# Flamingo block, latent attention: rotated query rows and folded matrix as two f16 parts, the partner sums placed a step earlier, the Exp table loaded ahead

## The reference, cut to what matters

```python
q_hk  = (hidden_q @ Wq.T).reshape(Bv, Sv, H, K)
q_big = einsum('bshk,hkq->bshq', q_hk, w_kc_q)
q_big = _apply_rope(q_big, sin_q, cos_q)        # x * cos + rotate_half(x) * sin
kv_r  = _apply_rope(kv_c, sin_k, cos_k)
q_r   = einsum('bshq,hqr->bhsr', q_big, W_qr)
k_r   = einsum('bld,hdr->bhlr', kv_r, W_kr)
attn  = softmax(einsum('bhsr,bhlr->bhsl', q_r, k_r), axis=-1)
ctx_c = einsum('bhsl,bld->bhsd', attn, kv_r)
ctx   = einsum('bhsd,hkd->bhsk', ctx_c, w_kc_kv)   # then @ Wo.T
```

## Time and profile before

| | |
|---|---|
| median of 3 runs | 469.99 us (468.45 to 471.33) |
| the profiled execution, its time | 470.19 us |
| its span, first to last instruction | 468.4 us |
| mean granted TensorE clock | 0.989 |
| first layer with its loads | 0 to about 144 us |
| attention | about 144 to 360 us |
| experts | about 360 to 468 us |

### The profile page before, as it was taken

How to read it: one execution, slowest core, us unless ns; L and a number is a source line. 1 busy time by engine, 2 the same in 40 slices (tenths; PEclk the granted TensorE clock), 3 DMA queues, 4 the chain that set the end, 5 groups by cost and what they waited for, 6 DMA issues and landing times. The chain is left out here.

```text
span 468.4 us, 8841 instructions
## 1 busy us (share of the span) xinstructions
PE 431.7 (92%) x2723; PEld 275.3 (59%) x2723; DVE 305.8 (65%) x886; ACT 251.6 (54%) x628; POOL 187.7 (40%) x190
## 2 busy tenths in 40 slices
PE   5895999989988999999999999999998997899997
PEld 2574777776744655555555555555565863644476
DVE  3989799964266767667775766867643759446612
ACT  3593436445335767776677676676665241145500
POOL 3450304040516546565555646545633006444000
PEclk9996999999999999999999999999999999999999
DMA  7733000000105233433424343212200898588202
GB/s 247 220 94 98 3 0 2 1 1 22 47 0 131 65 94 78 108 90 75 100 74 110 75 99 86 67 45 58 56 2 1 241 309 251 163 185 255 68 29 91
DMA packets 61448, 43.81 MB, mean 94 GB/s; under 512 B 22955, under 2 KB 54502, under 8 KB 61414
## 3 DMA queue, kind: packets, MB, share of 16 engines
q1 hardware_dynamic: 60646, 41.04, 32.9%
q0 software_dynamic: 768, 2.36, 2.5%
HBM read 27.25 MB, written 2.23 MB: 63 GB/s over the span
## 5 line engine op out<-in xcount | busy, mean ns | idle before, releaser
L1200 POOL TENSOR_TENSOR W1T<-W1T,inv 128x512 f32<-128x512 f32 x64 | 66.5, 1039 | 76.1 <-DVE inv L1250 75.8
L1144 ACT ACTIVATE W1T<-ps,low 128x256 f32<-128x256 f32 x128 | 59.5, 470 | 29.5 <-DVE low L1244 29.5
L275 POOL TENSOR_TENSOR rot<-rot 128x512 f32<-128x512 f32 x48 | 61.0, 1271 | 30.5 <-DMA rot<-rot 30.3
L1244 DVE TENSOR_REDUCE low<-ps 128x2 f32<-128x512 f32 x64 | 44.1, 689 | 39.6 <-PE ps L1062 39.1
L1070 PE MATMUL ps<-ident,W1T 128*128 128x128 f32 x256 | 41.1, 283 | 2.4 <-POOL W1T L1200 1.6
L1070 PEld LDWEIGHTS ps<-ident,W1T 128*128 128x128 f32 x256 | 27.7, 141 | 25.3 <-issue 20.3
L1152 ACT ACTIVATE W2T<-ps 128x512 f32<-128x512 f32 x64 | 38.2, 597 | 7.9 <-PE ps L1070 5.9
L255 DVE TENSOR_TENSOR rot<-ps,sinq 128x512 f32<-128x512 f32 x48 | 33.2, 691 | 13.3 <-PE ps L242 11.2
L242 PE MATMUL ps<-XH,CH 128*128 128x512 f16 x96 | 36.4, 379 | 0.9 <-DVE XL L859 0.9
L242 PE MATMUL ps<-XL,CH 128*128 128x512 f16 x96 | 36.4, 379 | 0.0
L242 PE MATMUL ps<-XH,CL 128*128 128x512 f16 x96 | 36.4, 379 | 0.0
(11 more groups left out here) (246 smaller groups left out, 867.2 us busy)
## 6 DMA issues: line engine op xcount, KB each, us to landing
rot<-rot SPq DMA_DIRECT2D x64, 128.0 KB, 2.3
rot<-rot SPq DMA_DIRECT2D x64, 64.0 KB, 2.0
EGU<-in_L_ffn_W_gate_dram SPq DMA_DIRECT2D x8, 384.0 KB, 5.7
EGU<-in_L_ffn_W_up_dram SPq DMA_DIRECT2D x8, 384.0 KB, 5.8
ED<-in_L_ffn_W_down_dram SPq DMA_DIRECT2D x8, 384.0 KB, 5.8
rot<-in_L_ffn_W_dram SPq DMA_DIRECT2D x2, 1024.0 KB, 8.1
WQ<-in_L_xattn_Wq_dram SPq DMA_DIRECT2D x8, 256.0 KB, 2.9
WO<-in_L_xattn_Wo_dram SPq DMA_DIRECT2D x8, 256.0 KB, 3.1
```

Source lines behind the costliest of these rows:

```text
L275: pool.tensor_tensor(g.RO[:, n, x, :], g.RO[:, n, x, :], g.TC[x][:, :], ALU.add).then_inc(g.sum_ok, 1)
L1144: e = act.activation(PB[t % 2][:, h, :], g.ps[:, SC + t % 2, h * S:(h + 1) * S], ACT.Exp, bias=low[:, t % 2, h:h + 1], scale=-1.0, accum_o ...
L1200: pool.tensor_tensor(PB[t % 2][:, :, :], PB[t % 2][:, :, :], inv[:, t % 2, :].unsqueeze(2).broadcast_to([P, 2, S]), ALU.mult).then_inc(nor ...
L1244: dve.tensor_reduce(low[:, t % 2, :], g.ps[:, SC + t % 2, :].rearrange("p (h s) -> p h s", h=2), AX.X, ALU.min).then_inc(low_ok, 1)
```

## The change

- Folded matrix: fold 4 joins `FOLD_SPLIT`; M is kept as two f16 parts MH and ML, scaled by UP = 64. ACT writes MH, and DVE (POOL in the first layer) the rest. In the stage DVE does it in step 7, behind the last inverse.
- Query rows: the sum of a group stands in RS, which has room for three groups and not six. ACT copies it to f16 (`rotated_high`, into RH), POOL subtracts that from RS and writes the f16 rest (`rotated_low`, into RL, in the space of XN).
- Context product: three terms (high x high, high x low, low x high) in f16 where one f32 product was. The factor 1/(UP UP) is taken out when the result is kept and when its rest is taken, for which DVE now uses scalar_tensor_tensor.
- A swap waits for `ro_low` of the group that had its place in RS, three groups earlier, and no longer for the context product.
- Order in the steps: sum 2 moves from step 4 to 3, sum 3 stays in 5, sum 4 in 6, and sum 5 goes from step 0 of the next pair to step 7. In steps 3 and 7 the low of an earlier group stands in front of the sum, in steps 4 and 6 the lows stand behind. ACT does high 0 and 1 in step 3, high 2 at the start of step 5 ahead of the exponentials, high 3 and 4 in step 7, high 5 at the start of step 1 of the next pair. POOL does low 5 in step 0, behind the normalisation.
- First layer's end: high and low of groups 0 to 2 are added on ACT and POOL, the first context product stands behind fold 0, and ACT issues an exponential of one element, with its table load, behind the first context keep.
- `bn_aggr` counts on the semaphore of `bn_stats`.

```diff
-FOLD_SPLIT = (0, 1, 5)
+FOLD_SPLIT = (0, 1, 4, 5)
...
     if f == 4:
-        return act.activation(g.M[u][:, :, :], o[:, 0:QT * DC], ACT.Copy, scale=1.0 / UP)
+        return act.activation(g.MH[u][:, :, :], o[:, 0:QT * DC], ACT.Copy, scale=UP)
...
-ROPE0, QC0, QCPS0, SUM0 = 2, 1, 2, QT
+ROPE0, QC0, QCPS0, SUM0, LOW0 = 2, 1, 2, QT, QT
...
     sp.wait_ge(g.sin_ok, GROUPS_Q * q + (k + 1))
-    sp.wait_ge(g.qc_ps, 2 * q + (n - 1 + QCPS0))
+    sp.wait_ge(g.ro_low, GROUPS_Q * q + (k - QT + 1 + LOW0))
...
-    pool.tensor_tensor(g.RO[:, n, x, :], g.RO[:, n, x, :], g.TC[x][:, :], ALU.add).then_inc(g.sum_ok, 1)
+    pool.tensor_tensor(g.RS[:, x, :], g.RS[:, x, :], g.TC[x][:, :], ALU.add).then_inc(g.sum_ok, 1)
+
+
+def rotated_high(act, g, q, k):
+
+    n, x = k // QT, k % QT
+    act.wait_ge(g.sum_ok, GROUPS_Q * q + (k + 1 + SUM0))
+    act.wait_ge(g.qc_ps, 2 * q + (n - 1 + QCPS0))
+    act.activation(g.RH[:, n, x, :], g.RS[:, x, :], ACT.Copy).then_inc(g.ro_high, 1)
+
+
+def rotated_low(pool, g, q, k):
+
+    n, x = k // QT, k % QT
+    pool.wait_ge(g.ro_high, GROUPS_Q * q + (k + 1))
+    pool.tensor_tensor(g.RL[n][:, x, :], g.RS[:, x, :], g.RH[:, n, x, :], ALU.subtract).then_inc(g.ro_low, 1)
 
 
 def context_product(pe, g, q, u, n):
 
-    pe.wait_ge(g.sum_ok, GROUPS_Q * q + (QT * n + QT + SUM0))
+    pe.wait_ge(g.ro_low, GROUPS_Q * q + (QT * n + QT + LOW0))
     pe.wait_ge(g.qc_ok, 2 * q + (n + QC0))
-    for h in range(2):
-        pe.matmul(g.ps[HI[h], QP, :], g.M[u][:, h, :], g.RO[:, n, h, :], start=True, stop=False)
-    for h in range(2):
-        mm = pe.matmul(g.ps[HI[h], QP, :], g.M[u][HI[h], 2, :], g.RO[HI[h], n, 2, :], start=False, stop=True)
+    terms = split(g.MH[u], g.ML[u], g.RH[:, n], g.RL[n])
+    for m, (mx, rx) in enumerate(terms):
+        for h in range(2):
+            pe.matmul(g.ps[HI[h], QP, :], mx[:, h, :], rx[:, h, :], start=(m == 0), stop=False)
+    for m, (mx, rx) in enumerate(terms):
+        for h in range(2):
+            mm = pe.matmul(g.ps[HI[h], QP, :], mx[HI[h], 2, :], rx[HI[h], 2, :], start=False, stop=(m == 2))
     mm.then_inc(g.qc_ps, 1)
...
                 if b == B - 1 and n >= 1:
                     add_partners(pool, g, 0, n - 1)
+                    if n == 1:
+                        rotated_low(pool, g, 0, 0)
+        for k in range(1, QT):
+            rotated_low(pool, g, 0, k)
...
         pe.wait_ge(gelu_ok, UNITS * B)
-        context_product(pe, g, 0, 0, 0)
         pe.wait_ge(x2_ok, 2 * B)
         pe.wait_ge(g.attention.credit, 1)
         next_fold(0)
+        context_product(pe, g, 0, 0, 0)
         second_norm(B - 1)
...
+                if b == B - 1 and n == 2:
+                    rotated_high(act, g, 0, 0)
+        for k in range(1, QT):
+            rotated_high(act, g, 0, k)
         norm_root(act, g, n2, B - 1)
...
         context_keep(act, g, 0, 0, 0)
+        act.activation(primed[:, :], g.gate[0:1, 0:1], ACT.Exp)
...
-    SUMMED = {1: 0, 2: 1, 4: 2, 5: 3, 6: 4}
+    SUMMED = {1: 0, 2: 1, 3: 2, 5: 3, 6: 4, 7: 5}
+    LOW_FIRST = (3, 7)
+    HIGH = {3: (0, 1), 7: (3, 4)}
+    LOW = {3: (0,), 4: (1, 2), 6: (3,), 7: (4,)}
...
         def step(p, u, t, asks, folds):
+            if asks and t == 5:
+                rotated_high(act, g, p + 1, QT - 1)
             softmax(p, t)
...
             if folds and t >= 3:
                 fold(p + 2, u, t - 3)
+            if asks:
+                for k in HIGH.get(t, ()):
+                    rotated_high(act, g, p + 1, k)
...
         def cross(p, u, t, asks, folds):
 
+            if t == 1:
+                rotated_high(act, g, p, GROUPS_Q - 1)
             softmax(p, t)
...
         def step(p, u, t, asks, folds):
             normalise(p, t)
-            if asks and t in SUMMED:
-                summed(p + 1, SUMMED[t])
+            if asks:
+                if t in SUMMED and t not in LOW_FIRST:
+                    summed(p + 1, SUMMED[t])
+                for k in LOW.get(t, ()):
+                    rotated_low(pool, g, p + 1, k)
+                if t in LOW_FIRST:
+                    summed(p + 1, SUMMED[t])
...
         def cross(p, u, t, asks, folds):
             step(p, u, t, asks, folds)
             if t == 0:
-                summed(p, GROUPS_Q - 1)
-
-        for k in range(QT, GROUPS_Q):
-            summed(0, k)
-        pairs(pool, step, cross)
+                rotated_low(pool, g, p, GROUPS_Q - 1)
+
+        summed(0, QT)
+        for k in range(QT, GROUPS_Q - 1):
+            summed(0, k + 1)
+            rotated_low(pool, g, 0, k)
+        pairs(pool, step, cross, head)
...
             inverse(p, t)
+            if folds and t == LAST:
+                fold(p + 2, u, FOLDS - 2)
```

More of the change, by code:

```diff
@@ L71, in norm_stats @@
     for t in range(n * q, n * q + n):
-        dve.wait_ge(nm.stats, t + 1)
-        dve.bn_aggr(g.mv[:, t, :], g.stat[:, t, :]).then_inc(nm.aggr, 1)
-    dve.wait_ge(nm.aggr, n * q + n)
+        dve.wait_ge(nm.stats, n * q + t + 1)
+        dve.bn_aggr(g.mv[:, t, :], g.stat[:, t, :]).then_inc(nm.stats, 1)
+    dve.wait_ge(nm.stats, 2 * n * (q + 1))
     dve.tensor_scalar(g.var[:, n * q:n * q + n], g.mv[:, n * q:n * q + n, 1], LN_EPS, None,
@@ L177, in fold_keep, with fold_parts @@
     if f == 4:
-        return act.activation(g.M[u][:, :, :], o[:, 0:QT * DC], ACT.Copy, scale=1.0 / UP)
+        return act.activation(g.MH[u][:, :, :], o[:, 0:QT * DC], ACT.Copy, scale=UP)
     return act.activation(g.NH[:, bass.ds(r, 1), :], o[:, 0:D], ACT.Copy, scale=UP)
+def fold_parts(g, r, u, f):
+    if f < 2:
+        return g.CH[u][:, f, :], g.CL[u][:, f, :], 2 * DQ
+    if f == 4:
+        return g.MH[u][:, :, :], g.ML[u][:, :, :], QT * DC
+    return g.NH[:, r, :], g.NL[:, r, :], D
 def fold_rest(dve, g, r, u, f, o):
-    hi, lo, w = ((g.CH[u][:, f, :], g.CL[u][:, f, :], 2 * DQ) if f < 2 else
-                 (g.NH[:, bass.ds(r, 1), :], g.NL[:, bass.ds(r, 1), :], D))
+    hi, lo, w = fold_parts(g, bass.ds(r, 1), u, f)
     return dve.scalar_tensor_tensor(out=lo, in0=o[:, 0:w], scalar=UP, in1=hi, op0=ALU.mult, op1=ALU.subtract)
@@ L292, in context_keep @@
     for h in range(2):
-        act.activation(g.Q[h][u][HI[h], 512 * n:512 * n + 512], g.ps[HI[h], QP, :], ACT.Copy).then_inc(g.qc_hi, 1)
+        act.activation(g.Q[h][u][HI[h], 512 * n:512 * n + 512], g.ps[HI[h], QP, :], ACT.Copy,
+                       scale=1.0 / (UP * UP)).then_inc(g.qc_hi, 1)
 def context_rest(dve, g, q, u, n):
@@ L300, in context_rest @@
     for h in range(2):
-        m = dve.tensor_tensor(g.Q[h][u][HI[1 - h], cols], g.ps[HI[h], QP, :], g.Q[h][u][HI[h], cols], ALU.subtract)
+        m = dve.scalar_tensor_tensor(out=g.Q[h][u][HI[1 - h], cols], in0=g.ps[HI[h], QP, :], scalar=1.0 / (UP * UP),
+                                     in1=g.Q[h][u][HI[h], cols], op0=ALU.mult, op1=ALU.subtract)
     m.then_inc(g.qc_ok, 1)
@@ L344, in stage_first_layer @@
     FS = sb("FS", [P, 2 * DQ])
+    primed = sb("exp_primed", [1, 1])
     FILL = 8 - TOP_BLK
@@ L430, in _ @@
         pool.memset(g.ident[:, :], 0.0).then_inc(id_zero, 1)
-        for start, v in ((g.rope_ok, ROPE0), (g.qc_ok, QC0), (g.qc_ps, QCPS0), (g.sum_ok, SUM0)):
+        for start, v in ((g.rope_ok, ROPE0), (g.qc_ok, QC0), (g.qc_ps, QCPS0), (g.sum_ok, SUM0),
+                         (g.ro_low, LOW0)):
             pool.sem_inc(start, v)
@@ L643, in first_queries @@
             pe.wait_ge(xl_ok, 2)
-            pe.wait_ge(fold_b, 2)
+            pe.wait_ge(fold_b, len(FOLD_SPLIT))
             pe.wait_ge(g.rope_ok, k + ROPE0)
@@ L1005, in stage_latent_attention, with pairs @@
     LAST = NT - 1
-    def pairs(eng, step, cross):
+    def pairs(eng, step, cross, head=None):
         for t in HEAD:
-            step(0, 0, t, True, False)
+            (head or step)(0, 0, t, True, False)
         with eng.Fori(0, (PAIRS - 2) // 2, 1) as it:
@@ L1172, in step, with head @@
                 turned(p, t - 1)
+        def head(p, u, t, asks, folds):
+            for k in range(QT, GROUPS_Q):
+                if t == min(1, k - QT):
+                    rotated_high(act, g, 0, k)
+            step(p, u, t, asks, folds)
         def cross(p, u, t, asks, folds):
+            if t == 1:
+                rotated_high(act, g, p, GROUPS_Q - 1)
             softmax(p, t)
@@ L1186, in _ @@
             fold(1, 1, f)
-        pairs(act, step, cross)
+        pairs(act, step, cross, head)
         turned(PAIRS - 1, LAST)
@@ L1205, in step, with head @@
             normalise(p, t)
-            if asks and t in SUMMED:
-                summed(p + 1, SUMMED[t])
+            if asks:
[5 more added lines that the diff above has]
+                    summed(p + 1, SUMMED[t])
+        def head(p, u, t, asks, folds):
+            step(p, u, t, asks, folds)
+            if t == 0:
+                rotated_low(pool, g, 0, GROUPS_Q - 1)
         def cross(p, u, t, asks, folds):
@@ L1949, in build @@
             g.CH, g.CL = two("CH", [P, KT, 2 * DQ], F16), two("CL", [P, KT, 2 * DQ], F16)
```

(8 more changed lines are left out.)

14 lines of the change are left out of this document (7 added, 7 removed).

## The result

The changed kernel is slower. Its median is 477.91 us (476.40 to 478.89, four runs), that of the kernel before, timed beside it, 470.66 us (468.45 to 471.70, four runs): ratio 1.0127, 95% interval 1.0086 to 1.0169. Medians are over all executions; the ratios leave out executions in a slower state, over 1.5% above the fastest of the same kernel. The prediction, 468.6 us with a range of 461 to 475, is wrong in size and in sign.

What follows compares the result with a forecast made beforehand. PE's order of work was taken to bound the attention stage. Inner pairs -4.7, start +0.5 and last transition +2.8 gave -1.4 us, so 468.6 us from a profiled 470.19, range 461 to 475.

Steps and rivals of the forecast that it cites:

- start, pair 0, steps 0 to 2: Start of the attention stage: POOL's new low parts delay the first transposes and product, less the product's saving; +0.5 us.
- six inner pairs, step 3 to step 2: Inner attention pairs, step 3 to the next pair's step 2: shorter products less a stall; -0.79 us each, -4.7 in sum.
- last transition, pair 6 from step 3 on: From pair 6 to 7, without folds: steps are shorter, so three stalls outweigh two shorter products; +2.8 us.
- The stall in step 6: Inner pair, step 6: PE's context product waits for POOL's f16 rest of query group 2; 0.55 us.
- low(k) and high(k): Per query group k, 0 to 5: POOL's f16 rest, 1.16 us, and ACT's f16 copy, 0.6 us.
- Rival D: Context product: column halves don't run side by side in f16, or all twelve loads are paid; +8.6, 479 us; 6%.
- The cap on a pair: Inner pair: gain at most 0.67 plus 0.2 us, since the partner-row add of group 4 waits for its late DMA.
- turn(0): PE's four transposes of tile 0; in pair 0 due 1.1 us later, because a low part delays tile 0's scaling.
- Exp table: First layer's end: loading the Exp table early is worth nothing; 0.2 us at most if it were not covered.
- rival C: Attention stage: partner-row adds moved ahead of scalings expose late DMA landings; 10 us over seven pairs, 478 us; 9%.
- turn(7): PE's four transposes of tile 7, inner pair: due at 257.28, just after POOL's scaling of it at 257.2.
- The first layer and the expert layer just slide: Outside the attention stage: the change adds or moves nothing that sets an end, so both only shift in time.

Runs made afterwards that it cites:

- e2: Kernel before with only its context product exchanged for twelve f16 matmuls on stand-in data; 465.29 us, ratio 0.990 to before.
- e4: Changed kernel with ACT's high copies cut to 16 of 512 columns, low parts at full length from other data; 475.31 us, ratio 1.0071 to before.
- e3: Changed kernel with POOL's low part of group 1 moved from step 4 to step 3; 474.00 us, ratio 1.0029 to before.
- e8: e3 without the weight loads of pairs 3 to 7 in the pair loop and the waits for them; 471.26 us, one run.
- e5: e3 with the sum of group 5 put back behind the scaling of tile 0 in the last transition; 470.60 us, ratio 0.9982 to before.
- e9: Changed kernel without the one-element Exp at the first layer's end, so the table loads in its old place; 476.54 us, ratio 1.0137 to before.
- e6: e3 with pair 0's low part of group 4 put behind the first scaling of tile 0; 473.33 us, ratio 1.0035 to before.
- e7: e3 with the edits of both e5 and e6; 471.77 us, ratio 0.9976 to before.

## Why the prediction was wrong

By the prediction's own three terms, in us, each measured from the first scores of one tile to those of another:

```
                                          predicted   measured
start, pair 0, steps 0 to 2               +0.5        +1.75
six inner pairs, step 3 to step 2         -4.7        +0.14
last transition, pair 6 from step 3 on    +2.8        +2.81
sum                                       -1.4        +4.7
```

**The step that failed most is the sum of an inner pair, -0.79 us six times.** Its mechanism was right, two of its sizes were not. The product was to take 1.35 us and takes 1.54 (the gaps at a change of tile are 0.1 us twice, where I had put 0.05 once, and the first rows are 0.24 apart). That is 0.48 gained, not 0.67, as e2 shows alone. The stall in step 6 was to be 0.55 us and is 0.7: low(2) ends at 252.70 and the product starts at 252.94, 0.24 later, where I had put 0.05. An inner pair follows: 2 x 0.48 - 0.7 = 0.26, measured 0.25, instead of 0.79. Over six pairs that is 3.2 us of the 6.1 between my -1.4 and the measured +4.7 of the attention stage.

**low(k) and high(k)** were put at 1.16 and 0.60 us and measured 1.159 and 0.628; the scaling from a narrower row held. The cost of ACT, nothing, held for the inner pairs (e4). Rival D fell: the halves run side by side.

**The cap on a pair.** An inner pair was to gain no more than 0.67 plus 0.2 us, because sum(4) comes late whatever PE does. In e3 pairs 2 and 5 gain 0.93 and 0.96 with low parts of full length, so this cap was too low; what the late sum(4) does cost shows in pairs 1, 3 and 4 of e3 and hangs on SP's queue, as I had it (e8).

**The start.** turn(0) was to be later by 1.1 us and is by 0.70: low(4) costs its 1.1, and the last transfer of group 5 landed 0.4 us earlier against the scores. At the full clock the start is +0.3 (e5, 9.04 us against 8.73) instead of +0.5. **The last transition**: stalls of 1.1, 1.2 and 1.85 predicted, 1.08, 1.2 and 1.31 measured. That the total is right to 0.1 us is luck: the two products save 0.4 less than I took, and the last stall is 0.5 shorter. (The 1.2 was a small slip: 329.65 and two lows of 1.16 give 331.97 and not 331.85, so by my own numbers 1.3.) **Exp table**: nothing, held (e9).

**What was not in the sum at all.** First, the clock. I took the full granted clock of the earlier trace rows for the changed kernel, though I had myself worked out that PE would stand still longer at the start. In the profiled execution a stretch at half clock follows that wait. It is worth 1.4 us: steps 0 to 2 of pair 0 take 10.48 us with it and 9.04 in e4 and e5 without (e3 against e5: 1.5). Second, the late landing, rival C: it came once, in pair 2, for 1.2 us, and not in all seven pairs; "+10 us" was far too much for it, and 0 in the forecast too little. The point from which it decides was 0.2 us per pair, and 1.2 in seven is just under that. Third, turn(7) of pair 0, due "just in time", waits for norm(7), 0.3 us. Together with the sizes above: 3.2 + 1.4 + 1.2 + 0.3 - 0.2 = 5.9 of the 6.1 us, where -0.2 is the start at the full clock.

The measured 477.9 us lies on the 478 of rival C and near the 479 of rival D. Neither is borne out by that: the landing cost 1.2 us and not 10, and the two halves of the product run side by side.

**"The first layer and the expert layer just slide."** They were 1.7 and 1.2 us longer in the profile. In front of pair 0 0.4 us of it is the change: the last fold waits 0.82 us for DVE's rest of fold 4 in every profiled kernel that has it, and 0.43 us for ACT in the kernel before and in e2. I had put that rest at nothing. The remainder is not shown to be the change: the start of pair 0 lies between 144.3 and 146.0 us in kernels with the same first layer (144.3 in e5, 146.0 in e8), and at 145.97 in e2, which has the old one. For the expert part, the two half-clock stretches there would by the price above more than account for it, but e9, with one of them, is at 112.2, and e6 at 119.0. The part varies by more than the change is worth. The profiles have two such stretches there against none, but the profiled execution of the kernel before is one with a clock that few of its executions have. Over whole executions the mean granted clock is 0.979 or less in all four of the changed kernel and in 19 of the 61 of the kernel before, so the changed kernel seems to meet more of them; what decides it is open. I tried nothing that sets PE's activity there apart from its waits.

So of the 7.3 us by which the median is slower, 4.7 are traced to the attention stage: POOL's queue (inner pairs, both ends), one late transfer and one half-clock stretch. Another 0.4 us, in front of pair 0, is DVE's rest of fold 4. The rest, 2.2 us, is where two executions of one program differ as well. The times by clock agree with this: the 16 executions of the kernel before with a mean clock of 0.978 have a median of 473.1 us, 4.8 less than the changed kernel's 477.9 at 0.975 to 0.979.

**A better version?** e7 takes 3.8 us off the attention stage compared with before and 8.5 compared with the changed kernel, and leaves nothing out. Its whole time is 0.9976 of before (0.9937 to 1.0015), no difference that these runs can tell. By the medians it beats the changed kernel by 6 us, and it doesn't beat the one before. The low part in another step is shown to help; that the f16 product pays in a kernel with a right result is not shown.

## What to carry to other kernels

A saving on the engine that binds is worth what the next engine's queue leaves of it: follow the order of that queue instruction by instruction, and put each new one where the engine already waits for something else; here one low part in another step was worth up to 0.7 us per pair, and one sum behind a norm 1.2 us. An instruction that waits for a DMA does not belong in front of one that the binding engine waits for, even when the transfer is in time in the profile: with no cushion, one landing 1 us late is lost in full. And where a sum of terms is 1.4 us in 470, price also what a wait can cost in the binding engine's clock, and look at several executions first, because a stage that the change doesn't touch moved by more than that.
